# Accumulating DMAs for identities, S1, U2 + S1 T1 and V2, and a new order of steps at the seam, in a two-layer LoRA kernel

## The reference

```
x = x + x @ W0.T + 0.5 * (x @ A0[i0[b]]) @ lora_B_w.T         # rank 32, 5 choices of A0
x = x + x @ W1.T + bias + 2.0 * (x @ A1[i1[b]]) @ B1[i1[b]]   # rank 16, 32 choices
```

## Time and profile before

| what | value |
|---|---|
| time, median of 3 runs | 302.75 us |
| time of the profiled execution | 301.54 us |
| span of its trace | 299.9 us |
| PE busy | 289.6 us (97%) |
| DVE, ACT, POOL busy | 194.2, 132.0, 57.9 us |
| chain that ended last, PE's share | 91% |

### The profile page before, as it was taken

One profiled execution on the slowest core, in us unless ns is written; L12 is line 12 of the kernel. 1 busy time (PEld: TensorE's weight loads), 2 busy tenths in 40 slices (PEclk: granted clock), 3 DMA queues, 4 the chain that ended last, 5 costly groups with the idle time before them and its releaser, 6 DMA issues.

```text
span 299.9 us, 3802 instructions
## 1 busy us (share of the span) xinstructions
PE 289.6 (97%) x1323; PEld 235.7 (79%) x1323; DVE 194.2 (65%) x298; ACT 132.0 (44%) x213; POOL 57.9 (19%) x78
## 2 busy tenths in 40 slices
PE   7999999999999996988999999999999999999995
PEld 2788777888788884867888888888888888888784
DVE  2789989999869999976465266256256256346120
ACT  3772235797590269236333433433423424414100
POOL 2500000500140100015160060160151151151000
PEclk9999999999999998999999999999999999999999
DMA  6998000200312005020825224324324324412003
GB/s 194 345 367 304 0 0 2 63 9 0 142 25 65 7 13 175 14 76 27 237 87 179 86 87 168 97 87 157 108 87 145 118 78 142 132 47 89 7 21 119
DMA packets 13750, 30.79 MB, mean 103 GB/s; under 512 B 2210, under 2 KB 3618, under 8 KB 12708
## 3 DMA queue, kind: packets, MB, share of 16 engines
q1 hardware_dynamic: 12708, 28.46, 28.1%
q0 software_dynamic: 1024, 2.10, 2.3%
HBM read 20.06 MB, written 8.39 MB: 95 GB/s over the span
## 4 chain that ended last, share of the span: by engine, by line
PE 91%; DVE 3%; ACT 2%; POOL 1%; DMA 1%; issue 1%; SPq 0%; DVEq 0%; ACTq 0%
PE bank L961 49%; PE bank L859 7%; PE bank L832 6%; PE bank L836 6%; PE bank L841 6%; PE bank L951 4%; PE bank L968 2%; PE bank L967 2%; PE bank L905 2%; PE bank L874 2%; DMA rA<-w 1%; PE bank L931 1%; ACT zo L437 1%; DVE X L604 1%; DVE zo L797 1%
## 5 line engine op out<-in xcount | busy, mean ns | idle before, releaser
L437 ACT ACTIVATE zo<-bank 128x512 f32<-128x512 f32 x32 | 19.1, 597 | 80.8 <-PE bank L961 57.0
L797 DVE TENSOR_TENSOR zo<-bank,zo 128x512 f32<-128x512 f32 x32 | 22.1, 691 | 48.6 <-PE bank L968 27.6
L961 PE MATMUL bank<-MM,X 128*128 128x512 f32 x192 | 46.2, 389 | 0.0
L961 PEld LDWEIGHTS bank<-MM,X 128*128 128x128 f32 x192 | 35.9, 188 | 7.4
L961 PE MATMUL bank<-sb,SH 128*128 128x512 f32 x96 | 24.8, 410 | 2.8 <-ACT zo L437 2.8
L604 DVE TENSOR_TENSOR SH<-xraw,SH 128x512 fp32r<-128x512 f32 x32 | 24.5, 803 | 3.9 <-ACT SH L437 3.9
L604 DVE TENSOR_TENSOR X<-xraw,X 128x1024 fp32r<-128x1024 f32 x16 | 19.5, 1221 | 9.9 <-ACT X L437 9.9
L437 ACT ACTIVATE SH<-xraw 128x512 fp32r<-128x512 f32 x32 | 19.1, 626 | 14.9 <-PE bank L968 7.1
L961 PEld LDWEIGHTS bank<-sb,SH 128*128 128x128 f32 x96 | 19.1, 200 | 7.3 <-ACT zo L437 3.2
L342 POOL TENSOR_TENSOR xraw<-xraw 128x512 f32<-128x512 f32 x7 | 9.0, 1290 | 81.0 <-DVE X L604 81.0
L961 PE MATMUL bank<-sc,SH 128*128 128x512 f32 x96 | 23.4, 392 | 1.0 <-DVE zo L797 1.0
(11 more groups left out here) (181 smaller groups left out, 544.6 us busy)
## 6 DMA issues: line engine op xcount, KB each, us to landing
xraw<-xT SPq DMA_DIRECT2D x8, 1024.0 KB, 5.1
out<-zo SPq DMA_DIRECT2D x32, 256.0 KB, 2.0
rB<-w1T SPq DMA_DIRECT2D x16, 256.0 KB, 8.7
rA<-w SPq DMA_DIRECT2D x15, 256.0 KB, 8.9
Rraw<-Rg SPq DMA_DIRECT2D x16, 128.0 KB, 3.7
rawA<-la SPq DMA_DIRECT2D x8, 128.0 KB, 2.2
Rraw<-lbs POOLq DMA_DIRECT2D x16, 64.0 KB, 3.1
rawA<-las POOLq DMA_DIRECT2D x8, 64.0 KB, 5.5
```

What stands on the lines that cost most here:

```text
L437: return eng.activation(o, i, ACT.Copy, scale=scale)
L797: ins = eng.tensor_tensor(zo[z][:, :], bank[bk][:, :], zo[z][:, :], ALU.add)
L961: ins = mm(bk[:, :], x(px, k), m(pm, k), start=(start and n == 0 and k == 0), stop=(stop and n == 2 and k == H - 1), skip_group_check=True)
```

## The change

- Identities of A22 and B22 for k = 1 to 3, the four S1, the four U2P5 and the four V2 are no longer DVE sums: POOL issues a DMA for each that adds the source to the destination in SBUF (`accum_op=ALU.add`), with a semaphore of its own. Readers wait for that semaphore.
- In the DVE list these entries go; a low of V1 two rounds back takes RL's place in the loop over i, and a few lists at the seam are reordered: H of M21 0 to 2 come early, E1(0) stands between the two H of V2, SH and SL of batch 0 are spread out, RH, RL, M22, C22a, V4, C11 follow, and C22b and C12 of batch 0 come before the SLs of batch 1.
- Batch 0's steps on PE are P1, P5, P6, P2a, P7, P2, P3, D, P4, U. P2a is the first pass (4 matmuls) of the product with M21, P2 the other two passes and the low-rank pair.

```diff
-            return ["P1", "P5", "P6", "P2", "P7", "D", "P3", "P4", "U"]
+            return ["P1", "P5", "P6", "P2a", "P7", "P2", "P3", "D", "P4", "U"]
...
-        dve_prog += [("I", "A22", k), ("I", "B22", k), ("S3", k), ("T1", k), ("S2", k), ("T2", k)]
+        dve_prog += [("I", "A22", k), ("I", "B22", k)] if k == 0 else []
+        dve_prog += [("S3", k), ("T1", k), ("S2", k), ("T2", k)]
...
-        dve_prog += [("S1", k)] + l_([("T1", k, k + 1), ("S1", k, k + 1)])
+        dve_prog += l_([("T1", k, k + 1), ("S1", k, k + 1)])
...
-    dve_prog += l_(two("A22")) + [("A1DL",), ("WSL",)] + [("U2P5", i) for i in range(H)] + l_(two("B22"))
+    dve_prog += l_(two("A22")) + [("A1DL",), ("WSL",)] + l_(two("B22"))
...
     for i in range(H):
-        dve_prog += [("M12", i)] + ([("SA", 0, 2)] if i == 0 else [("SA", 0, 4)] if i == 1 else [("RL", 0)] if i == 2 else [])
-        dve_prog += [("V1", i), ("V3", i), ("V2", i)]
+        dve_prog += [("M12", i)] + ([("SA", 0, 2)] if i == 0 else [("SA", 0, 4)] if i == 1 else l_([("V1", i - 2, i - 1)]))
+        dve_prog += [("V1", i), ("V3", i)]
         act_prog += h([("V1", i, i + 1)])
-        if i > 0:
-            dve_prog += l_([("V1", i - 1, i)])
-        if i == 1:
-            act_prog += [("RH", 0)]
-    act_prog += [("SH", 0, n) for n in (1, 2, 3, 4)] + h(two("V3"))
-    dve_prog += [("SL", 0, 1)] + l_([("V1", 3, 4)]) + [("SL", 0, n) for n in (2, 3, 4)] + l_(two("V3"))
-    act_prog += h([("M21", 0, 1), ("M21", 1, 2), ("M21", 2, 3)] + two("V2") + [("M21", 3, 4)])
-    dve_prog += l_([("M21", 0, 1), ("M21", 1, 2), ("M21", 2, 3)] + two("V2") + [("M21", 3, 4)])
-    act_prog += [("UH", 0), ("E1", 0)] + h(two("M22"))
-    dve_prog += [("U2", 0), ("UT", 0), ("UL", 0)] + l_(two("M22")) + [("V4", i) for i in range(H)]
-
-    act_prog += [("aH", 1), ("gH", 1), ("xH", 1, 0), ("E2", 0)] + h([("V4", 0, 2)]) + [("E3", 0)] + h([("V4", 2, 4)])
+        act_prog += h([("M21", 0, 1)] if i == 1 else [("M21", 1, 2), ("M21", 2, 3)] if i == 2 else [])
+    act_prog += [("SH", 0, 1)] + h([("V3", 0, 2)]) + [("SH", 0, 2)] + h([("V3", 2, 4)])
+    dve_prog += l_([("V1", 2, 3)]) + [("SL", 0, 1)] + l_([("V1", 3, 4), ("V3", 0, 2)]) + [("SL", 0, 2)]
+    act_prog += h([("V2", 0, 2)]) + [("E1", 0)] + h([("V2", 2, 4)]) + h([("M21", 3, 4)])
+    dve_prog += l_([("V3", 2, 4)] + two("V2")) + [("SL", 0, 3)] + l_(one("M21")) + [("SL", 0, 4)]
+    act_prog += [("SH", 0, 3), ("SH", 0, 4), ("UH", 0), ("E2", 0), ("RH", 0)]
+    dve_prog += [("U2", 0), ("UT", 0), ("UL", 0), ("RL", 0)]
+
+    act_prog += h(two("M22")) + [("E3", 0), ("aH", 1), ("gH", 1)] + h([("V4", 0, 2)]) + [("xH", 1, 0)] + h([("V4", 2, 4)])
+    dve_prog += l_(two("M22")) + [("C22a", 0)] + [("V4", i) for i in range(H)] + [("C11", 0)] + l_(two("V4"))
     act_prog += [("xH", 1, 1)] + [("SH", 1, n) for n in range(1, 5)] + [("E4", 0), ("UH", 1), ("RH", 1)]
-    dve_prog += [("C11", 0)] + l_([("V4", 0, 2)]) + [("C22a", 0), ("C22b", 0)] + l_([("V4", 2, 4)])
-    dve_prog += [("aL", 1), ("gL", 1), ("xL", 1, 0), ("xL", 1, 1)] + [("SL", 1, n) for n in range(1, 4)]
-    dve_prog += [("C12", 0), ("SL", 1, 4), ("U2", 1), ("UT", 1), ("UL", 1), ("RL", 1)]
+    dve_prog += [("aL", 1), ("gL", 1), ("xL", 1, 0), ("C22b", 0), ("xL", 1, 1), ("C12", 0)]
+    dve_prog += [("SL", 1, n) for n in range(1, 5)] + [("U2", 1), ("UT", 1), ("UL", 1), ("RL", 1)]
...
+            def add(name, k, o, i):
+                eng.dma_start(o, i, accum_op=ALU.add).then_inc(d_sum[name, k], 16)
+
+            for k in range(H):
+                if k > 0:
+                    for q in ("A22", "B22"):
+                        eng.wait_ge(d_w[q, k, 0], 16)
+                        add("I_" + q, k, raw[q][:, k, 128 * k:128 * (k + 1)], ident[:, :])
+                    eng.wait_ge(d_sum["I_A22", k], 16)
+                eng.wait_ge(s_dve, dve_at["S3", k])
+                add("S1", k, raw["A21"][:, k, :], raw["A22"][:, k, :])
+
...
+            for k in range(H):
+                eng.wait_ge(s_act, max(act_at["U2s", k], act_at["P5s", k]))
+                add("U2P5", k, raw["A21"][:, k, :], raw["A22"][:, k, :])
...
                 elif op == "v0":
                     load_v(0)
+                    for k in range(H):
+                        eng.wait_ge(s_dve, max(dve_at["V3", k], L_at["M11", k]))
+                        add("V2", k, M11[:, k, :], raw["A21"][:, k, :])
...
+                    elif step == "P2a":
+                        eng.wait_ge(s_dve, dve_at["M12", ZBANK - H])
+                        product(bZ, xa2, m_("M21"), True, made("M21"), stop=False, passes=(0,))
+                        continue
                     elif step == "P2":
                         if b >= 1:
                             eng.wait_ge(s_dve, dve_at["C11", b - 1])
-                        else:
-                            eng.wait_ge(s_dve, dve_at["M12", ZBANK - H])
-                        product(bZ, xa2, m_("M21"), True, made("M21"), stop=False)
+                        product(bZ, xa2, m_("M21"), True, made("M21"), stop=False, passes=range(b == 0, 3))
                         eng.wait_ge(s_dve, dve_at["UL", b])
                         eng.wait_ge(s_dve, dve_at["RL", b])
                         ins = delta(bZ, b, TA, 0)
```

More of the change, by code:

```diff
@@ L75, in lora_kernel @@
     for b in range(B):
-        pe_names += [(n, b + 1) if n == "U" else (n, b) for n in batch_steps(b)]
+        pe_names += [(n, b + 1) if n == "U" else (n, b) for n in batch_steps(b) if n != "P2a"]
     pe_at = Order(pe_names).at
@@ L272, in lora_kernel @@
         d_z = [sem(f"d_z{i}") for i in range(4)]
+        d_sum = {(n, k): sem(f"d_{n}_{k}") for n in ("I_A22", "I_B22") for k in range(1, H)}
+        d_sum |= {(n, k): sem(f"d_{n}_{k}") for n in ("S1", "U2P5", "V2") for k in range(H)}
         pool_prog = ["id0", "ident", "mk0", "mk1", "mask", "wz"]
@@ L443, in wait_raw @@
                         eng.wait_ge(d_w[q, k, 0], 16)
-                if q in ("A11", "B11", "A22", "B22"):
-                    eng.wait_ge(s_dve, dve_at["I", q, hi - 1])
+                if q in ("A22", "B22"):
+                    for k in range(max(lo, 1), hi):
+                        eng.wait_ge(d_sum["I_" + q, k], 16)
+                if ("I", q, lo) in dve_at:
+                    eng.wait_ge(s_dve, dve_at["I", q, lo])
+                elif q in ("S1", "V2"):
+                    for k in range(lo, hi):
+                        eng.wait_ge(d_sum[q, k], 16)
+                elif q in ("A22", "B22"):
+                    pass
                 elif q[0] in "STV" or q in ("M11", "M22"):
@@ L643, in _ @@
                     eng.wait_ge(s_dve, dve_at["S3", i])
+                    if i > 0:
+                        eng.wait_ge(d_sum["I_A22", i], 16)
                     ins = eng.tensor_tensor(low["e"][:, i, :], raw["A22"][:, i, :], raw["A11"][:, i, :], ALU.subtract)
@@ L648, in _ @@
                     ins = eng.tensor_tensor(raw["A12"][:, i, :], raw["A12"][:, i, :], low["e"][:, i, :], ALU.subtract)
[L649 to L652, removed]
                 elif k == "T1":
@@ L659, in _ @@
                     i = op[1]
-                    eng.wait_ge(s_dve, max(dve_at["T1", i], dve_at["I", "B22", i]))
+                    eng.wait_ge(s_dve, max(dve_at["T1", i], dve_at["I", "B22", 0]))
+                    if i > 0:
+                        eng.wait_ge(d_sum["I_B22", i], 16)
                     ins = eng.tensor_tensor(low["f"][:, i, :], raw["B22"][:, i, :], raw["B11"][:, i, :], ALU.subtract)
@@ L669, in _ @@
                     ins = eng.tensor_tensor(raw["B21"][:, i, :], raw["B21"][:, i, :], low["f"][:, i, :], ALU.subtract)
-                elif k in ("M11", "M12", "M22", "U2P5"):
+                elif k in ("M11", "M12", "M22"):
                     i = op[1]
-                    p, bk, o = {"M11": ("m1", i, M11), "M22": ("m7", i, raw["A22"]), "U2P5": ("m5", H + i, raw["A21"]),
+                    p, bk, o = {"M11": ("m1", i, M11), "M22": ("m7", i, raw["A22"]),
                                 "M12": ("m3", H + i, raw["A21"])}[k]
@@ L676, in _ @@
                         eng.wait_ge(s_act, act_at["MZ", i])
[L677 to L681, removed]
+                    else:
+                        eng.wait_ge(d_sum["U2P5", i], 16)
                     ins = eng.tensor_tensor(o[:, i, :], bank[bk][:, :], o[:, i, :], ALU.add)
@@ L691, in _ @@
                     ins = eng.tensor_tensor(raw["A21"][:, i, :], raw["A22"][:, i, :], raw["A21"][:, i, :], ALU.subtract)
[L692 to L695, removed]
                 elif k == "V4":
                     i = op[1]
-                    eng.wait_ge(s_dve, dve_at["V2", i])
+                    eng.wait_ge(d_sum["V2", i], 16)
                     eng.wait_ge(s_dve, L_at["M22", i])
@@ L895, in _ @@
             by_rows("m7", [(s_act, act_at["U2s", i]) for i in range(H)], "S3", "T3", 0, False)
-            eng.wait_ge(s_dve, dve_at["U2P5", 0])
+            eng.wait_ge(s_act, act_at["P5s", 0])
```

(10 more changed lines are left out.)

## The result

The changed kernel takes 299.42 us (median of 20 runs, 298.18 to 301.24), the kernel before 301.38 in as many runs (299.91 to 303.88): ratio 0.9939, 95% interval 0.9922 to 0.9956, so 1.96 us or 0.6% faster. I had forecast 3.5 us less than 302.75, which is 299.2. The direction and the seam's mechanism came out; the gain is little more than half of the forecast, and three terms of the sum were off. The experiments show that the gain rests on the new order with its split product, and that most of the DMAs add nothing to it.

The account below looks back on a forecast made before the run. It took PE's waits at the seam, 7.35 us, as the loss, with DVE's queue the new bound. 302.75 less 3.5 (3.34 at P6(1), less 0.14 restart, plus 0.3 from m6) gave 299.2; range 295.8 to 301.8.

Parts of the forecast that it names:

- steps 1 to 7: From weight preparation's end into batch 1: new order followed through PE, ACT and DVE; P6(1) comes 3.34 us earlier.
- rival 2: In the new 1.6 us gap before U(1), PE's clock falls again, costing 1.7 us: 300.9; chance 0.11.
- The 0.3 of m6: PE's product m6, before the seam: two identities of k=3 off DVE let it run unhindered, gaining 0.3 us.
- Rival 4: Weight preparation: identity DMAs land late for S2[k]; slower than before from 8.0 us landing, 305.6 at 8.9; chance 0.06.
- the restart's 0.14: PE behind P6(1): restarting after the wait there costs 0.14 us, where before there was none.
- x(2)'s load: Batch 1: it follows SL(1,4) and lands 0.1 us before E2(1) is wanted, so no new loss counted.
- the fall of the clock: PE from P6(0) to P2(0): clock drops after 2.96 us idle, losing 1.72 us; gone in the new order.
- The accumulating DMAs' cost: DMAs that add in SBUF: 4 us to land in quiet time, 0.5 us of POOL per issue.
- So 4 us are freed on DVE in front of P5 and P6: Loop over i: without V2, DVE's rounds end at 104.4, where the last V2 had started at 108.33.
- rival 3: Seam: DVE's spared work isn't on the way to xL(1,1), P6(1) stays put, 302.4; chance 0.10.

Follow-up runs that it names:

- e10: e9 with the identities of k = 3 alone by DMA; 294.46 us, ratio 0.9778 to the kernel before.
- e11: The changed kernel run again without edit; 299.26 us, ratio 0.9939 to the kernel before.
- e2: The changed kernel with the four V2 back as DVE sums; 299.45 us, ratio 0.9942 to the kernel before.
- e4: The changed kernel with batch 0's product with M21 whole, ahead of P7; 300.97 us, ratio 0.9987 to the kernel before.
- e5: The changed kernel with H V2[2:4], H M21[3] and SH(0,3) ahead of E1(0) on ACT; 298.11 us, ratio 0.9905 to the kernel before.
- e6: The changed kernel with E1(1) ahead of SH(1,4), E4(0), UH(1) and RH(1) on ACT; 299.12 us, ratio 0.9943 to the kernel before.
- e8: The changed kernel with the two identities of k = 1 back on DVE; 298.27 us, ratio 0.9910 to the kernel before.
- e1: The kernel before run again without edit; 301.61 us, ratio 1.0003 to the kernel before.
- e7: The kernel before with the V2 sums by DMA and nothing else; 297.34 us, ratio 0.9881 to the kernel before.
- e9: e7 with the split product with M21, D behind P3 and reordered ACT and DVE queues; 294.31 us, ratio 0.9775 to the kernel before.

## Why the prediction was right or wrong

**The seam, steps 1 to 7: right.** Forecast -3.34 us at P6(1), measured -2.96 (35.59 to 32.63) in both traces of the changed kernel. Each new gap stands where it was put, held by what was named. The 0.38 is DVE's sums from L V2[2:4] to xL(1,1), 19.4 for 19.1, and their start, pushed by 0.07. The clock doesn't fall in the new gap of 1.45 us (rival 2 didn't come).

**299.2 against 299.42: luck.** The sum started from 302.75, the median of 3 runs; 20 runs gave 301.38, which is 1.37 lower. That hides most of the error in the gain, 3.5 for 1.96.

**The 0.3 of m6: wrong.** "so only the two identities of k=3, 0.4 us, move L("T2",3) forward. Gain: 0.3 us" failed for the change as it stands: it took the DMAs' landing in quiet time for k = 1 as well. For k = 3 alone it holds (e10). Rival 4 had the room right (5.9 us from issue) and the landing in the saturated stretch possible; it took 8.2, and DVE's pause of 2.5 ate what it had in hand. k = 2 and 3 landed in 3.1 to 3.4 us in quieter time, so the rival's sum over three rounds didn't come either. Where PE starts m6 as early as in the kernel before (38.96 in e11 as in the earlier trace rows), m6 takes 11.42 for 11.19: +0.23 instead of -0.3; in e2, e4 and e5, with the same identities and starts at 38.3 to 38.5, it takes 11.54, 11.07 and 11.85. In the first trace of the changed kernel it takes 10.88, because PE was 1.15 us late there from the start-up on and gave DVE time; in e6, later still, too.

**Behind P6(1): mis-sized.** I counted the restart's 0.14 and gave x(2)'s load 0.1 us of room. From P6(1) to the end of the span it takes 156.21 us against 155.89 in the kernel before, 0.32 more: the restart's 0.14, and 0.18 that I hadn't counted, nearly all of it in P7(1), whose matmuls take 3.03 for 2.88. In e11 both together are 0.23. That it is E2(1) which P7(1) waits for, is shown where the wait is long enough to be seen, as in e6 and e8.

**The median: mis-sized.** The sum was made against an execution with the fall of the clock. In 17 of 89 executions the kernel before doesn't have it and is 1.2 us faster, 0.22 us on the mean (by the mean clock, see e1).

Together: 3.5 - 0.38 - 0.53 - 0.18 - 0.22 = 2.2, against 1.96 measured (interval 1.3 to 2.35). The rest is within the interval. The 0.53 is e11's m6 and leans on one pair of traces. It isn't settled how much the start-up adds: P1(0) starts anywhere between 107.6 and 110.6 in the thirteen traces of all kernels.

**The accumulating DMAs' cost: right.** 3.6 and 4.0 us for 256 KB, where I took 4. The Trainium skill ("DMA: Bandwidth & Descriptors", Anatomy of one DMA) fits a DMA issued by GpSimd with 2.0 us plus the bytes at 436 GB/s; the estimate by it would be 2.6 us. The trace's 3.6 is above it, and the measurement stands.

**"So 4 us are freed on DVE in front of P5 and P6": nearly true, and without effect.** The prediction did not ask what V2's DMAs are worth in the new order, though its rival 3 had the reason: the steps that count begin at E1(0), which depends on PE. For V2 that rival came true (e2, 0.23 us); its price did not, since the order and the split carry the gain. In the old order V2 by DMA is worth 3.7 us (e7). The new order gives time away where ACT and DVE come to an operation too early and other work stands behind it: H V2[2:4] behind E1(0) and RH(0) behind E2(0), which e5 shows. That C11 and C22b ahead of xL(1,1) cost something too is argued; only e9, with all moves together, has them elsewhere.

## What to carry to other kernels

When several changes are made together, try each alone from both ends, added to the kernel before and taken out of the changed one. Here V2 off DVE, added alone, gains 1.2%; the new order without it (e2) gains 0.6%, and the two together gain 0.6% as well. Both take away the same wait before P6(0), and the order brings waits of its own. In hand-written queues, a copy that waits for a product must not stand ahead of work that doesn't: put it where its product is just done, and behind each wait removed look for the next operation that stands behind an evacuation. Price a DMA by the traffic at the time of its issue.
